# A two-layer gated block on one core: the shared stage of its expert layer in a new order, and three loads of the tile stage at another place

## What is computed

```python
def _L1_ffn_ref(x, ...):
    logits = x @ router_w.T
    probs = softmax(logits)
    topk_w, topk_idx = top_k(probs, 2)
    topk_w = topk_w / sum(topk_w)
    # every expert e: silu(x @ gate_w[e]) * (x @ up_w[e]) @ down_w[e], weighted by combine[:, e]
    shared = silu(x @ s_gate_w + s_gate_b) * (x @ s_up_w + s_up_b) @ s_down_w + s_down_b
    return moe_out + shared
x = x + tanh(g_ffn[1]) * _L1_ffn_ref(_layernorm(x), ...)
```

## Time and profile before

| | before |
|---|---|
| median of 3 runs | 1141.89 us (1140.69 to 1152.41) |
| span of the profiled execution | 1146.9 us |
| granted TensorE clock, mean | 0.962 |
| PE busy | 1028.8 us, 90% |
| DVE busy | 747.0 us, 65% |
| ACT busy | 601.8 us, 52% |
| POOL busy | 456.0 us, 40% |
| shared stage (PE) | 691.35 to 858.4 us |
| tile stage up to the last product of a tile | 860.6 to 1090.6 us |

### The profile page before, as it was taken

The page is one execution under the profiler, slowest core; times in us unless marked ns, Lnnn a source line. Parts: engine busy times, 40 slices in busy tenths (PEclk is TensorE's granted clock), DMA queues, the critical chain, the costliest instruction groups (busy, mean ns, idle before and its releaser), DMA issues. The chain is left out here.

```text
span 1146.9 us, 17729 instructions
## 1 busy us (share of the span) xinstructions
PE 1028.8 (90%) x5438; PEld 475.5 (41%) x5439; DVE 747.0 (65%) x1419; ACT 601.8 (52%) x898; POOL 456.0 (40%) x483
## 2 busy tenths in 40 slices
PE   0466889999789999999999998999998899999996
PEld 0243445555423223323322324455445455555542
DVE  6988988888786776578477547745545344443347
ACT  6897999999346776467467565452211111111110
POOL 1100335544410242243134341000657788889065
PEclk9978899999979999999999999998999899999998
DMA  9322930000534234134211004201678888976588
GB/s 325 114 74 80 342 138 1 2 1 9 133 89 107 80 82 116 62 58 94 66 48 44 12 21 136 76 26 52 243 282 170 200 205 207 206 192 146 153 284 291
DMA packets 174204, 142.39 MB, mean 124 GB/s; under 512 B 121364, under 2 KB 137108, under 8 KB 173624
## 3 DMA queue, kind: packets, MB, share of 16 engines
q1 hardware_dynamic: 163560, 110.40, 34.7%
q0 software_dynamic: 8672, 29.76, 7.9%
q10 hardware_dynamic: 1904, 1.38, 0.6%
HBM read 70.93 MB, written 43.37 MB: 100 GB/s over the span
## 5 line engine op out<-in xcount | busy, mean ns | idle before, releaser
L1432 ACT ACTIVATE prob<-p_col,mask_col,any_key 128x512 f32<-128x512 f32 x256 | 186.2, 781 | 103.2 <-PE p_col L1564 102.3
L1653 DVE CUSTOM_DVE_ANT_0 ajunk<-p_row,mask_row 128x512 bf16<-128x512 f32 x256 | 166.2, 686 | 64.1 <-PE p_row L1513 62.5
L1526 PE MATMUL p_out<-prob,v 128*64 128x512 f32 x512 | 138.1, 618 | 0.1
L1332 POOL TENSOR_TENSOR o<-sum_a,rec 32x512 f32<-32x512 f32 x30 | 39.1, 1304 | 186.1 <-DMA rec<-inv_d 184.0
L1513 PE MATMUL p_row<-ks,early_place 99*128 99x512 f16 x256 | 100.5, 395 | 8.7 <-DVE top L1653 8.0
L1564 PE MATMUL p_col<-early_place,ks 101*128 101x512 f16 x256 | 97.7, 385 | 0.9 <-ACT prob L1432 0.3
L2647 DVE SCALAR_TENSOR_TENSOR shid<-s_up,ssilu 128x352 f32<-128x352 f32 x39 | 20.4, 524 | 99.0 <-PE s_up L2565 98.8
L2513 ACT ACTIVATE ssilu<-s_gate 128x352 f32<-128x352 f32 x39 | 18.1, 463 | 124.0 <-PE s_gate L2565 124.0
L2578 PE MATMUL s_down<-mw,shT 128*128 (+1 forms) x351 | 82.0, 379 | 0.0
L2565 PE MATMUL s_gate<-mw,sxT 128*128 x444 | 74.1, 318 | 6.7 <-DMA sxT<-x_slots 6.7
L2565 PE MATMUL s_up<-mw,sxT 128*128 x444 | 73.5, 316 | 0.0
(11 more groups left out here) (354 smaller groups left out, 2077.3 us busy)
## 6 DMA issues: line engine op xcount, KB each, us to landing
x_slots<-nought SPq DMA_DIRECT2D x3, 3328.0 KB, 18.4
y_slots<-y SPq DMA_DIRECT2D x39, 256.0 KB, 2.2
early_place<-in_ctx SPq DMA_DIRECT2D x8, 1024.0 KB, 6.2
early_place<-halves_d SPq DMA_DIRECT2D x45, 128.0 KB, 2.5
halves_d<-halves SPq DMA_DIRECT2D x18, 256.0 KB, 2.1
mstg<-in_L_ffn_gate_w POOLq DMA_DIRECT2D x6, 704.0 KB, 5.7
mstg<-in_L_ffn_up_w POOLq DMA_DIRECT2D x6, 704.0 KB, 6.0
x<-in_x SPq DMA_DIRECT2D x4, 1024.0 KB, 7.3
```

The lines of the kernel that those rows point to most:

```text
L1432: nc.scalar.activation(prob[s % 4][:, c, :], p_col[c][:], ACT.Exp, bias=mask_col[:, b, k:k + 1], scale=any_key[:, b:b + 1]).then_inc(t_exp, 1)
L1526: mm = nc.tensor.matmul(p_out[pr][c * 2 * DH:(c + 1) * 2 * DH, :], v1[b % 2][:, k, g, :], prob[n % 4][:, c, :], start=(k == 0), stop=(k == ...
L1653: nc.vector.tensor_tensor_reduce(junk[:, n % 2, :], p_row[n % 2][:], mask_row[:, blk // HPG, :], 1.0, -3e38, ALU.add, ALU.max, top[blk % 2 ...
```

## The change

Rows of all batches are split earlier (two buffers xn). Batches 1 to 3 are no longer turned by PE and ACT but by DMA transposes that SP issues between its weight loads (turn_rows, semaphores m_turned). The router stands within the second batch's first gate/up half, number_slots within its second half, and the choice is cut into probabilities, best_two, choose and shares, spread over DVE's work there. The scatter's rows are let go in steps behind given products (SCATTER_AFTER). The stores of the shared weights and of late_d are issued ahead of the loads of the parts from (2, 2) on. SP turns the first four tiles of x_slots in the shared stage, not two, and the tile stage's own loads begin with tile 4. ACT's three loads of shared weights go out behind tile 29 (r = 14, n = 1), not behind tile 3.

```diff
+SCATTER_AFTER = [("up", n) for n in (11, 12)] + [("down", n) for n in (10, 12)] + [("up", n) for n in (13, 13, 14, 14, 15)] + \
+    [("down", n) for n in (13, 14, 15, 16)] + [("up", n) for n in (16, 17, 17)]
...
+FIRST = 4
...
+            def turn_rows(*tiles_):
+                for t in tiles_:
+                    b = t // TPB
+                    if t % TPB == 0:
+                        sp.wait_ge(m_xl, b)
+                    sp.dma_start_transpose(xT[:, :, :, t * P:(t + 1) * P].rearrange("p h k s -> p (h k) s"), row_of(t)).then_inc(m_turned[b - 1], 16)
+
+            weights(1, 0)
+            weights(1, 1)
+            turn_rows(4, 5)
+            weights(0, 2)
+            turn_rows(6)
+            weights(0, 3)
+            turn_rows(7)
+            weights(1, 2)
+            turn_rows(8, 9)
+            weights(1, 3)
+            turn_rows(10, 11, 12, 13, 14, 15)
+            weights(2, 0)
+            weights(2, 1)
             for u in range(2):
...
-            sp.wait_ge(m_xT, NT)
+            sp.wait_ge(m_turned[LATE_B - 1], 16 * TPB)
             for h in range(2):
                 sp.dma_start(late_d[h], xT[:, h, :, LATE_B * S:(LATE_B + 1) * S]).then_inc(m_saved, 16)
+            for u, q in ORDER[8:]:
+                weights(u, q)
             sp.wait_ge(m_turn, TPB)
             sp.wait_ge(m_scat, SCATTERED)
-            for n in range(2):
+            for n in range(FIRST):
...
+                    if 2 * t + s in pace:
+                        done, count = pace[2 * t + s]
+                        pool.wait_ge({"up": m_up, "down": m_down}[done], count)
...
-            hidden(0, 0, lambda: high(1), lambda: high_parts(1, 0, 1), lambda: high_parts(0, 2, 3))
+            def high_next():
+                high_parts(1, 0, 1)
+                high(2)
+
+            hidden(0, 0, lambda: high(1), high_next, lambda: high_parts(0, 2, 3))
             act.wait_ge(m_rwt, 1)
             nc.scalar.copy(rwT[0][:], p_rw).then_inc(m_rwh, 1)
-            turned(4)
-            turned(5)
-            high(2)
-            hidden(0, 1, lambda: high_parts(1, 2, 3))
-            for t in range(6, 10):
-                turned(t)
-            high(3)
+            hidden(0, 1, lambda: None, lambda: None, lambda: high(3))
+            high_parts(1, 2, 3)
             act.wait_ge(m_const, CONSTS)
             hidden(1, 0, lambda: high_part(2, 0), lambda: high_part(2, 1))
-            for t in range(10, NT):
-                turned(t)
             act.wait_ge(m_shift, 1)
             nc.scalar.activation(logit[:], logit[:], ACT.Exp).then_inc(m_exp, 1)
-            hidden(1, 1, lambda: high_part(2, 2), lambda: high_part(2, 3))
+            hidden(1, 1, lambda: None, lambda: high_part(2, 2), lambda: high_part(2, 3))
...
-                    need(pe, m_xl, t // TPB)
...
-                    pe.wait_ge(m_xT, TPB * (g + 1))
+                    pe.wait_ge(*((m_turned[g - 1], 16 * TPB) if g else (m_xT, TPB)))
                 for m in range(EB):
+                    if 0 < m <= len(between):
+                        between[m - 1]()
...
             gate_up(0, 0)
             turn_router()
-            turn(4, 5)
             gate_up(0, 1)
-            turn(6, 7)
             down(0, 0)
-            turn(8, 9)
-            gate_up(1, 0)
-            turn(10, 11)
-            down(0, 1, 12, 13)
-            turn(14, 15)
-            router()
-            gate_up(1, 1)
+            gate_up(1, 0, lambda: None, router)
+            down(0, 1)
+            gate_up(1, 1, number_slots)
             down(1, 0)
...
-            for n in range(2):
-                for h in range(2):
-                    low_piece(n, h)
+            low_piece(0, 0)
+            low_piece(0, 1)
             normalise(1)
+            low_piece(1, 0)
+            low_piece(1, 1)
+            statistics(2)
...
+            def first_rows():
+                low_rows(1)
+                normalise(2)
+
+            def second_rows():
+                low_rows(2)
+                dve.wait_ge(m_b, 16)
+                nc.vector.tensor_scalar(bias_dg[:], bias_dg[:], gates[:, 3:4], None, ALU.mult)
+
+            def third_rows():
+                statistics(3)
+                normalise(3)
+
+            hidden(0, 0, first_rows, lambda: low_parts(1, 0, 1), lambda: low_parts(0, 2, 3))
             dve.wait_ge(m_rwh, 1)
             nc.vector.tensor_tensor(rwT[1][:], p_rw, rwT[0][:], ALU.subtract).then_inc(m_rwl, 1)
             link(nc.vector.tensor_scalar(gate_dn[:], gates[:, 3:4], 1.0 / W_UP, None, ALU.mult))
-            statistics(2)
-            normalise(2)
-            dve.wait_ge(m_b, 16)
-            nc.vector.tensor_scalar(bias_dg[:], bias_dg[:], gates[:, 3:4], None, ALU.mult)
-            low_rows(2)
-            hidden(0, 1, lambda: low_parts(1, 2, 3), lambda: statistics(3))
-            add(0, 0)
-            normalise(3)
+            hidden(0, 1, second_rows, third_rows)
+            add(0, 0, 0, 2)
             low_rows(3)
-            hidden(1, 0, lambda: low_part(2, 0), lambda: low_part(2, 1))
-            add(0, 1)
+            add(0, 0, 2, TPB)
+            low_parts(1, 2, 3)
+            hidden(1, 0, lambda: low_part(2, 0), lambda: low_part(2, 1), probabilities)
+            best_two()
+            add(0, 1, 0, 2)
             choose()
-            hidden(1, 1, lambda: low_part(2, 2), lambda: low_part(2, 3))
+            add(0, 1, 2, TPB)
+            shares()
+            hidden(1, 1, find_slots, lambda: low_part(2, 2), lambda: low_part(2, 3))
             add(1, 0)
...
+    LATE_LOADS_AT = PAIRS_OF_TILES - 4
...
-                load(2 + n, n)
+                load(FIRST + n, n)
...
-            for n in range(2):
-                body(0, n, False)
-            with sp.Fori(1, PAIRS_OF_TILES - 1) as r:
+            for r in range(FIRST // 2):
+                for n in range(2):
+                    body(r, n, False)
+            with sp.Fori(FIRST // 2, PAIRS_OF_TILES - 1) as r:
...
-            act.wait_ge(e_up, 2)
+            with act.Fori(2, LATE_LOADS_AT) as r:
+                for n in range(2):
+                    body(r, n)
             nc.scalar.dma_start(first_gate, shared_d[0, :, :, G0:U0]).then_inc(e_pre, 16)
             for h in range(2):
                 nc.scalar.dma_start(first_up[:, h, :, :], shared_d[0, :, h, U0:D0].rearrange("p (k i) -> p k i", i=EI)[:, :, 0:P]).then_inc(e_pre, 16)
-            with act.Fori(2, PAIRS_OF_TILES) as r:
+            with act.Fori(LATE_LOADS_AT, PAIRS_OF_TILES) as r:
```

More of the change, by code:

```diff
@@ L1800, in stage_experts @@
     m_wa, m_wb, m_wh, m_wl = (sem("m_" + n) for n in ("wa", "wb", "wh", "wl"))
-    m_first = [sem(f"m_first{n}") for n in range(2)]
-    first_xT = keep[:].rearrange("p t c -> p (t c)")[:, 0:2 * 2 * KB * P].rearrange("p (n h k t) -> p n h k t", n=2, h=2, t=P)
+    m_first = [sem(f"m_first{n}") for n in range(FIRST)]
+    first_xT = keep[:].rearrange("p t c -> p (t c)")[:, 0:FIRST * 2 * KB * P].rearrange("p (n h k t) -> p n h k t", n=FIRST, h=2, t=P)
     with ExitStack() as inner:
@@ L1869, in stage_shared @@
     assert AT_XT + 2 * KB * NTOK * 2 <= SHARED * SLOT
-    xn = place(0, TPB * D * 4, F32).rearrange("p (t d) -> p t d", d=D)
+    xn = [place(n * TPB * D * 4, TPB * D * 4, F32).rearrange("p (t d) -> p t d", d=D) for n in range(2)]
     number_i = place(SLOT, NT * EXPERTS * 4, mybir.dt.int32).rearrange("p (t e) -> p t e", e=EXPERTS)
@@ L2097, in router @@
                 pe.wait_ge(m_rwl, 1)
-                pe.wait_ge(m_xT, NT)
+                for done in m_turned:
+                    pe.wait_ge(done, 16 * TPB)
                 for t in range(NT):
@@ L2245, in hidden_low, with add @@
                                                hT[n][0][0:rows(m), m, :], ALU.mult, ALU.subtract).then_inc(m_hl, 1)
-            def add(g, n):
-                for t in range(TPB):
+            def add(g, n, t0=0, t1=TPB):
+                for t in range(t0, t1):
                     dve.wait_ge(m_down, TPB * (2 * g + n) + t + 1)
@@ L2384, in first, with ahead @@
         return isinstance(r, int) and r == 0
-    def last(r):
-        return isinstance(r, int) and r == PAIRS_OF_TILES
+    def ahead(r):
+        return isinstance(r, int) and 2 * r < FIRST
     with nc.Block() as block:
@@ L2584, in body @@
                 e = expert(i)
-                pe.wait_ge(*((m_first[n], 16) if first(r) else (e_xin[n], 16 * r)))
+                pe.wait_ge(*((m_first[i], 16) if ahead(r) else (e_xin[n], 16 * (r - (FIRST // 2 - 1)))))
                 pe.wait_ge(m_wl, NQ * e + (NQ * 3 + MORE))
```

30 lines of the change are left out of this document (14 added, 16 removed).

## The result

The changed kernel takes 1140.61 us (median of 19 runs, 1135.89 to 1146.82) where the kernel before takes 1146.39 (19 runs beside them, 1140.69 to 1156.71). The ratio is 0.9945, 95% interval 0.9922 to 0.9967: 6.3 us less by the ratio, 5.8 by the medians. Forecast were 1134.0 us and a range of 1126 to 1140. The time lies 0.6 us above that range, and the largest term of the forecast's tile stage came out far smaller.

The account below looks back on a forecast made before the run. PE, busy 90% of the span, was taken as the bound. Gains of 3.7 us in the shared stage and 4.2 in the tile stage, 7.9 in sum, took 1141.89 to 1134.0 us, range 1126 to 1140.

Parts of the forecast that it names:

- Shared stage: 3.7 us forecast: Shared stage, net: 11.2 us removed, less 4.8 of new stalls and 2.7 of slow groups; between 2.8 and 6.4 us.
- stalls of 2.6 and 2.2 us: Shared stage: PE would wait for two DVE adds, each behind two down tiles, 4.8 us in sum.
- slow groups of 1.8 and 0.9: Shared stage: slow work behind the new stalls, charged whole for the longer and half for the other, 2.7 us.
- The router's wait: Shared stage, ahead of the router: PE's wait of 1.66 us for ACT's eviction of tile 15 would go.
- The DMA turns: Batch 3's four turns would land at 746.8, before the router asks at 750.7: hidden, with 3.9 us to spare.
- Tile stage: 4.2 us forecast: Tile stage, net: 9.4 us gained, less 0.8 for POOL and 4.4 for ACT's late loads.
- the wait of 6.37 us and the slow groups go: 9.4 us: Start of the tile stage, tile at 892.72: its wait for transposed rows and 3.1 us of slow groups would vanish.
- POOL: 0.8 us forecast: Tile 27: PE would wait 0.8 us, hand-over included, for POOL's weight split of expert 6.
- Late loads: 4.4 us forecast: Behind tile 29: ACT's moved loads would delay a turn, 2.6 us stall plus 1.8 slow groups; bounds 0 and 8.6.
- rival A: Tile stage: late loads fit into the DMA engines' free third; gain 12.3 to 15.0 us, time 1127 to 1129.6; chance 0.25.
- rival B: Tile stage: the old stall only moves to tile 30, both shared stalls cold; gain 2.8 us, time 1139; chance 0.20.
- the same 7.9 us give 1134.0: Whole kernel: the summed gain taken from the earlier runs' median of 1141.89 us, 5 us under the profiled span.

Follow-up runs that it names:

- the two repetitions: Changed kernel and kernel before, each run again with one register operation more per tile on PE: 1140.81 us (ratio 0.9935) and 1146.88 us (0.9996).
- The run with this part alone: Changed kernel with two tiles turned ahead and ACT's three loads at their old place, leaving the shared stage's new order: 1140.09 us, ratio 0.9942.
- the tile-only one: Kernel before with four tiles turned ahead and ACT's loads behind tile 29, on the old shared stage: 1148.39 us, ratio 1.0013.
- the late-loads kernel: Kernel before with only ACT's three loads of shared weights moved behind tile 29: 1187.18 us, ratio 0.9994, against 1188.67 us on that chip.
- The kernel with both improvements: Changed kernel with DVE's adds in a new order and POOL's first two loads issued in the shared stage: 1131.19 us; 1154.27 us on the slow chip.

## Why the prediction went as it did

**Shared stage: 3.7 us forecast, 4.4 by the profile (5.5 between the two repetitions).** The mechanism was right, and the terms held nearly: stalls of 2.6 and 2.2 us forecast, 2.26 and 2.23 found; slow groups of 1.8 and 0.9 forecast, 1.7 and 1.7 found here, and 0 and 1.7 in the repetition. The router's wait is gone, and its slow follower takes 4.46 us instead of 5.28, which the sum had left alone. (The 1.75 us of the old slow group set a duration against a time from start to start; from start to start it is 732.37 - 728.19 - 2.59 = 1.6.) The DMA turns were hidden. The run with this part alone confirms it: it carries the whole gain of the change.

**Tile stage: 4.2 us forecast, 1.4 by the profile, none by the experiment.** The step that failed is "the wait of 6.37 us and the slow groups go: 9.4 us". It took one long wait of one execution for a fixed cost of ACT's loads. In its repetition the same kernel waits 0.69 us at tile 5 and 4.4 in sum at tiles 5, 6 and 8, and without POOL's loads ACT's make turned rows land after 6.2 us and stop PE nowhere. The edits took about 2.5 us of waits away near tile 5, not 6.4, and in the changed kernel POOL let none of it through. The sum of the waits for transfers over the stage is 0 to 13 us from execution to execution.

**POOL: 0.8 us forecast, 3.3 and a slow group of 1.7 found.** The forecast put expert 6 ready 2.2 us sooner than the earlier trace rows, because POOL's wait of that size would go, and took the rest of POOL's pace as fixed. It is not: in the profiled executions expert 2 was ready at 34.8 us before and 34.3 after, but each further expert took 28.9 us before, 29.9 after, and 24.3 without POOL's loads. Counted from tile 0, expert 6 was ready at 150.5 us in the profiled execution before, at 153.0 in its repetition, and at 150.9 to 155.7 in the eight other executions that load as before. A margin of 6.7 us read off one execution was really one of 1.1 to 6.6 (tile 27 started at 154.1 in the repetition), so POOL's pace capped the tile stage's gain at tile 27, whatever is done to the transfers ahead of it: at 3.1 us between the profiled executions, at 0.4 between the repetitions.

**Late loads: 4.4 us forecast, 0 found in the changed kernel, 4.9 and a slow group in the tile-only one.** Of rival A it came true that the late loads fitted in, of rival B that a long wait stood behind them, in different executions; neither's sum did. The form "one value with two bounds" hid that this cost changes from execution to execution and is not an unknown constant.

**The base.** The sum by spans was 7.9 us forecast and 7.8 found, but that is luck: it is 0.7 too little in one stage and 2.8 too much in the other, and the other 2.0 us lie outside both (0.9 ahead of PE's first product of the shared stage, 0.1 at the border, 0.9 behind the start of tile 38). Against the medians the gain is 5.8. The step that put the time outside the range is "the same 7.9 us give 1134.0": it took the median of three runs, 1141.89, for the kernel's own time, although its profiled span lay 5 us above it. Nineteen runs give 1146.39. From there the same sum gives 1138.5, within 2.1 us of the result, with the errors of the two stages still in it.

**The range.** The forecast's bounds let the cases differ by their costs only. The executions of the one kernel spread over 16.0 us and those of the other over 10.9, more than any term.

## What to carry to other kernels

A wait for a transfer in one trace shows that transfers meet, not which one is to blame: before it is priced as removable, see whether it stands in a second execution, and leave out each stream in turn, the largest too and not the nearest alone. Where an engine works on its own clock ahead of the bound engine (POOL's split here), write down for each hand-over when it is ready and when it is asked for: the smallest margin caps what anything ahead of it can gain, and starting that engine's first load earlier was worth 4.6 us, more than the two edits aimed at the stalls. A base time needs as many runs as its spread asks for; three are too few for half a per cent.

## What the runs showed of the chip

SP's issue of a turn, 1.2 us as a rule, took 5.09 us at 925 in the changed kernel, while the last turn of hidden values was 11.6 us on its way: the crowded moment held the issuing engine as well.

One of the chips ran all kernels longer, the kernel before at 1188.7 us. PE's timeline of the late-loads kernel there:

```profile
845.15 0.38 PE L2133 MATMUL p_up<-mw 128*96 128x512 f16 x1 [1.70 <-issue]
846.55 0.58 PE L2133 MATMUL p_up<-mw 128*96 128x512 f16 x1 [1.02 <-issue]
...
855.69 16.64 PE L2151 MATMUL p_down<-mw 96*128 96x512 f16 x66 [0.86 <-issue]
```

From 843 to 856 us, and again from 1124 to 1150, PE issues single products 1.4 to 3.5 us apart and waits for nothing that the profile shows. The granted clock is 0.79 over 843 to 875. The shared stage takes 173.9 us there, where the repetition of the kernel before on another chip has 161.3. The kernel with both improvements had no such stretch in its shared stage (149.3 us), only one in its tail, and came out at 0.971 of the kernel before. Why the one is held in that stage and the other not was not tried.
